# A two-layer graph network with residual norms on one core: the table of edge counts built inside the first 16 blocks of layer 0, its dense products in the next 25, staging by ScalarE and VectorE

## The reference

```python
# layer 0: graph convolution with self loops
deg  = segment_sum(1, dst) + 1;  dinv = rsqrt(deg)
h    = segment_sum(dinv[src] * dinv[dst] * (x @ W)[src], dst) + dinv**2 * (x @ W) + b
x    = layernorm(x + h + t_emb @ Wt + bt)
# layers 1 and 2: two sage convolutions, the second on relu of the first
mean = segment_sum(h[src], dst) / max(cnt, 1)
h    = mean @ Wl.T + h @ Wr.T + b
x    = layernorm(x + h2)
```

## Time and profile before

| what | value |
|---|---|
| median of 3 runs | 3074.04 us (3073.63 to 3077.73) |
| the profiled execution | 3073.91 us |
| its span, first to last instruction | 3072.1 us |
| mean granted TensorE clock | 0.965 |
| PE busy | 2648.3 us, 86% |
| POOL busy | 1972.9 us, 64% |
| DVE busy | 1115.7 us, 36% |
| ACT busy | 557.2 us, 18% |
| DMA, mean over the span | 209 GB/s |

### The profile page before, as it was taken

One profiled execution on the slowest core, in us unless ns is written; L12 is line 12 of the kernel. 1 busy time (PEld: TensorE's weight loads), 2 busy tenths in 40 slices (PEclk: granted clock), 3 DMA queues, 4 the chain that ended last, 5 costly groups with the idle time before them and its releaser, 6 DMA issues.

```text
span 3072.1 us, 53544 instructions
## 1 busy us (share of the span) xinstructions
PE 2648.3 (86%) x9848; PEld 988.0 (32%) x9849; DVE 1115.7 (36%) x2442; ACT 557.2 (18%) x1268; POOL 1972.9 (64%) x2061
## 2 busy tenths in 40 slices
PE   7567788888888988999999998988988889989988
PEld 6321222222222333333333323333333333333323
DVE  8771222334454521122223333332222223334444
ACT  0130111111222211111112112221111111222222
POOL 1247777777776646556667777746555656777774
PEclk9998999999999999999999999999999999999999
DMA  5247777777777756667778888866656667777775
GB/s 188 92 162 210 209 219 220 221 223 225 226 227 217 211 164 194 196 205 212 222 222 250 252 255 251 257 221 200 178 169 181 193 189 206 224 225 227 232 216 162
DMA packets 223328, 641.67 MB, mean 209 GB/s; under 512 B 38526, under 2 KB 40144, under 8 KB 223270
## 3 DMA queue, kind: packets, MB, share of 16 engines
q0 software_dynamic: 161280, 528.61, 59.4%
q1 hardware_dynamic: 46356, 84.02, 7.5%
q10 hardware_dynamic: 15666, 28.72, 2.8%
HBM read 589.84 MB, written 52.15 MB: 209 GB/s over the span
## 4 chain that ended last, share of the span: by engine, by line
PE 61%; issue 12%; DVE 8%; POOL 6%; DVEq 5%; DMA 5%; ACT 2%; ACTq 1%; POOLq 0%; SPq 0%
PE sum_ps L1241 26%; PE prod_ps L1235 13%; PE root_ps L1252 13%; POOL raw L534 6%; PE dense_ps L1268 4%; DMA raw<-table,idx_ring 3%; ACT half_sum L1015 2%; PE selfT_ps L1280 1%; DVE oh L875 1%; PE root_ps L1121 1%; DVE X L805 1%; DMA raw<-rows,idx_ring 1%; DVEq L318 1%; DVEq L312 1%; DVE oh_key L766 1%
## 5 line engine op out<-in xcount | busy, mean ns | idle before, releaser
L534 POOL DMA_INDIRECT raw<-rows,idx_ring x1344 | 1280.9, 953 | 692.1 <-issue 452.0
L1241 PE MATMUL sum_ps<-raw,oh 128*64 128x512 f32 x4032 | 1001.7, 618 | 145.1 <-DVE oh L875 67.7
L534 POOL DMA_INDIRECT raw<-table,idx_ring x672 | 640.5, 953 | 230.1 <-issue 183.2
L1235 PE MATMUL prod_ps<-W,aggT 128*128 128x512 f32 x1176 | 553.8, 614 | 15.1 <-issue 10.1
L1241 PEld LDWEIGHTS sum_ps<-raw,oh 128*64 128x64 f32 x4032 | 273.9, 140 | 765.2 <-issue 760.4
L1252 PE MATMUL root_ps<-W,selfT 128*128 128x512 f32 x800 | 405.9, 654 | 120.6 <-DVE X L789 67.4
L1015 ACT ACTIVATE half_sum<-sum_ps 64x512 f32<-64x512 f32 x294 | 174.4, 593 | 1234.3 <-PE sum_ps L1246 1234.3
L1241 PE MATMUL sum_ps<-raw,oh_next 128*64 128x512 f32 x1176 | 317.2, 618 | 5.9 <-DVE oh_next L854 5.7
L1235 PEld LDWEIGHTS prod_ps<-W,aggT 128*128 128x128 f32 x1176 | 218.0, 196 | 238.4 <-issue 236.2
L875 DVE TENSOR_TENSOR oh<-iota_ps,dst_rel 128x512 f32<-128x512 f32 x253 | 173.7, 687 | 311.3 <-PE sum_ps L1241 281.3
L817 DVE TENSOR_TENSOR agg<-sum_ps,half_sum 64x512 f32<-64x512 f32 x147 | 100.3, 683 | 504.5 <-ACT half_sum L1015 493.1
(11 more groups left out here) (209 smaller groups left out, 1425.2 us busy)
## 6 DMA issues: line engine op xcount, KB each, us to landing
selfbuf<-rows ACTq DMA_DIRECT2D x103, 256.0 KB
raw<-rows,idx_ring POOLq DMA_INDIRECT x1344
rows<-X SPq DMA_DIRECT2D x49, 256.0 KB
rows<-hbuf SPq DMA_DIRECT2D x49, 256.0 KB
X<-rows SPq DMA_DIRECT2D x49, 256.0 KB
out<-X SPq DMA_DIRECT2D x48, 256.0 KB
table<-stage SPq DMA_DIRECT2D x21, 512.0 KB, 3.3
raw<-table,idx_ring POOLq DMA_INDIRECT x672
```

What stands on the lines that cost most here:

```text
L534: nc.gpsimd.indirect_dma_start(out=raw[:, n, j, :], out_offset=None, in_=tables[L][:, :], in_offset=bass.IndirectOffsetOnAxis(ap=idx_ring[ ...
L1235: last = mm(product(L, t1), aggT[:, k * P:(k + 1) * P], W[:, 0, k, :], start=(k == 0), stop=(k == KD - 1))
L1241: return mm(sum_ps[j * H:(j + 1) * H, bank:bank + D], of[:, j, :], raw[:, n, j, :], start=fresh, stop=False, skip_group_check=True)
```

## The change

- The counting leaves the prologue. In each of blocks 0 to 15 of layer 0 (`i < COUNT_BLOCKS`), DVE makes and PE multiplies the batches of two windows, one before each half, into `root_ps` and `dense_ps` by turns, and ScalarE reads them out there.
- The dense products of layer 0 come in blocks 16 to 40, one before each half: 50, the last on a tile of zeros. They take `table0`'s rows (dinv·x) from `selfbuf`, which ScalarE loads by DMA, and `counts` unscaled. The table `rooted` is not read in layer 0.
- POOL stages nothing; DVE stages the 21 tiles, behind its tables of window ends, with `ranges`, `tile_end_counts`, `biases` and `column_numbers` put in between. ScalarE stages without a stop, but for the edge tables after the sixteenth of its 28 tiles.
- The scratch of the counting shares its room with the second weight matrix, now a tensor of its own (`W_right`). SP loads that matrix when the counting is over, after 24 tiles of layer 0 are stored.
- CAP goes from 32 to 23: fewer columns (161, not 216) can hold edges of the first 128 targets. The number of edges is the same.

```diff
-    CAP = 32
+    CAP = 23
+    COUNT_BLOCKS = DW // 2
+    DENSE_BLOCKS = -(-T // 2)
+    OWN0 = 2 * DENSE_BLOCKS
...
+        def early_blocks(eng, i, count_part, dense_part):
+            with eng.If(i < COUNT_BLOCKS):
+                count_part(nc.s_assert_within(i, 0, COUNT_BLOCKS - 1, skip_runtime_bounds_check_because="asked just here"))
+            with eng.Else():
+                with eng.If(i < COUNT_BLOCKS + DENSE_BLOCKS):
+                    dense_part(nc.s_assert_within((i - COUNT_BLOCKS) & 31, 0, DENSE_BLOCKS - 1,
+                                                  skip_runtime_bounds_check_because="asked just here"))
+                eng.nop()
+            eng.nop()
...
# SP
-            load_weights(1, wr1t, "wr_loaded")
+            with sp.Fori(0, T // 2) as t:
+                store_x(t)
+            sp.wait_ge(S["c_taken"], DW + 2)
+            load_weights(1, wr1t, "wr_loaded")
...
# POOL: its staging loop is gone
             b0 = first_block(pool)
             pool.wait_ge(S["b0_all_ps"], 1)
+            pool.wait_ge(S["ranges_made"], 1)
+            pool.wait_ge(S["tabs_made"], 2)
...
# DVE
+            for n, (first, many) in enumerate(TWOS):
+                b = first // BT
+                if b >= 2 and first % BT == 0:
+                    dve.wait_ge((S["stage_stored0"], S["stage_stored1"])[b % 2], 16 * PAIRS * (b // 2))
+                if many == 2:
+                    t = first + 1
+                    v.tensor_scalar(stage[:, b % 2, t % BT, :], X[:, t, :], dinv[:, t:t + 1], None,
+                                    ALU.mult).then_inc(S["staged_dve"], 1)
+                if n == 8:
+                    ranges()
+                if n == 10:
+                    tile_end_counts()
+                if n == 16:
+                    biases()
+                if n == 20:
+                    column_numbers()
             relative_targets()
...
+            def count_edges(i, half):
+                first = dense_bounds(mybir.EngineType.DVE, dense_first, i * 2 + half)
+                shift = dense_bounds(mybir.EngineType.DVE, dense_shift, i * 2 + half)
+                batches(dve, first[0], first[1], lambda g: dense_batch(i * 2 + half, g, shift[0]))
...
                     for half in range(2):
                         if L > 0:
                             each(dve, rounds[half], rounds[half + 1], lambda r: own_rows(L, r), T + 1)
+                        else:
+                            with dve.If(i < COUNT_BLOCKS):
+                                count_edges(...)
+                            dve.nop()
                         each(dve, ends[half], ends[half + 1], window_end)
                         half_block(...)
...
                     dve.wait_ge(S["stage_stored1"], 16 * 3 * PAIRS)
+                    dense_columns()
...
# ScalarE, in each half of layer 0's blocks
+                    def taken(i):
+                        take_counts(i * 2 + half, (root_ps, dense_ps)[half])
+                        if half == 1:
+                            with act.If(i > COUNT_BLOCKS - 2):
+                                first_counts()
+                            act.nop()
+                    def ahead(d):
+                        if half == 0:
+                            tile_ahead(d * 2 + 1)
+                        else:
+                            with act.If(d < DENSE_BLOCKS - 1):
+                                tile_ahead(d * 2 + 2)
+                            act.nop()
+                    early_blocks(act, i, taken, ahead)
...
+            def next_tile(t1):
+                act.dma_start(selfbuf[:, :], table0[rows_of(t1), :]).then_inc(S["self_loaded"], 16)
+                next_counts(t1)
+            def tile_ahead(done):
+                act.wait_ge(S["dense_done"], done)
+                next_tile(...)
...
# PE, in each half of layer 0's blocks, ahead of its four groups
+            def count_window(w, bank, first, end):
+                pe.wait_ge(S["c_taken"], w + 1)
+                clear(bank, KEYS)
+                batches(pe, first, end, lambda g: count_pairs(bank, g))
+                mm(bank[:, 0:1], zeros[:, :], zeros[:, 0:1], start=False, stop=True,
+                   skip_group_check=True).then_inc(S["c_ready"], 1)
...
+            def first_layer_dense(d, half):
+                t1 = d * 2 + (1 + half)
+                pe.wait_ge(S["self_loaded"], t1 * 16)
+                pe.wait_ge(S["cbuf_ready"], t1)
...
+                    add_dense(selfbuf[:, :], False).then_inc(S["dense_done"], 1)
```

More of the change, by code:

```diff
@@ L1022, in own_rows @@
                 act.dma_start(selfbuf[:, :], rows32[L - 1][rows_of(r + 2), :]).then_inc(S["self_loaded"], 16)
-                next_counts(nc.s_assert_within(r + 2, 1, CTILES, skip_runtime_bounds_check_because="two tiles ahead"), L)
-            def first_layer_counts(r):
-                with act.If(r < T):
-                    act.wait_ge(S["dense_done"], r)
-                    next_counts(nc.s_assert_within(r + 1, 1, T, skip_runtime_bounds_check_because="not the last tile"), 0)
-                act.nop()
+                next_counts(nc.s_assert_within(r + 2, 1, CTILES, skip_runtime_bounds_check_because="two tiles ahead"))
             def deviation(L, t1):
@@ L1234, in weigh @@
                 for k in range(KD):
-                    last = mm(product(L, t1), aggT[:, k * P:(k + 1) * P], W[:, 0, k, :], start=(k == 0),
+                    last = mm(product(L, t1), aggT[:, k * P:(k + 1) * P], W[0][:, k, :], start=(k == 0),
                               stop=(k == KD - 1))
@@ L1251, in by_weights @@
                 for k in range(KD):
-                    last = mm(out_ps, xT[:, k * P:(k + 1) * P], W[:, n, k, :], start=(k == 0),
+                    last = mm(out_ps, xT[:, k * P:(k + 1) * P], W[n][:, k, :], start=(k == 0),
                               stop=(k == KD - 1))
@@ L1268, in add_dense @@
                 return mm(dense_ps[:, :], cbuf[:, :], rows, start=fresh, stop=False, skip_group_check=True)
-            def first_layer_dense(r):
-                with pe.If(r < T):
-                    t1 = nc.s_assert_within(r + 1, 1, T, skip_runtime_bounds_check_because="not the last tile")
-                    pe.wait_ge(S["cbuf_ready"], t1)
-                    add_dense(tile_of_x(t1), False).then_inc(S["dense_done"], 1)
-                pe.nop()
+            def first_layer_dense(d, half):
+                t1 = d * 2 + (1 + half)
+                pe.wait_ge(S["self_loaded"], t1 * 16)
+                pe.wait_ge(S["cbuf_ready"], t1)
+                if half == 0:
+                    with pe.If(d > 0):
+                        add_dense(selfbuf[:, :], False).then_inc(S["dense_done"], 1)
+                    with pe.Else():
+                        add_dense(selfbuf[:, :], True).then_inc(S["dense_done"], 1)
+                    pe.nop()
+                else:
+                    add_dense(selfbuf[:, :], False).then_inc(S["dense_done"], 1)
             def transpose_own(rows):
@@ L1301, in _, with first_layer_half, count @@
                         transpose_own(selfbuf)
+                def first_layer_half(i, half):
+                    def count(i):
+                        first = nc.values_load_multi_w_load_instructions(
+                            dense_first[0:1, bass.ds(i * 2 + half, 2)], engines=[mybir.EngineType.PE], min_val=0, max_val=GMAX,
+                            skip_runtime_bounds_check_because="counts of batches, bounded by the capped number of edges")[1]
+                        count_window(i * 2 + half, (root_ps, dense_ps)[half], first[0], first[1])
+                    early_blocks(pe, i, count, lambda d: first_layer_dense(d, half))
                 def groups(i, b):
                     ends = ended_before(mybir.EngineType.PE, b * SLOTS, SLOTS)
-                    rounds = rooted_before(mybir.EngineType.PE, b)
+                    if L > 0:
+                        rounds = rooted_before(mybir.EngineType.PE, b)
                     for n in range(SLOTS):
-                        if n % HR == 0:
-                            each(pe, rounds[n // HR], rounds[n // HR + 1],
-                                 first_layer_dense if L == 0 else lambda r: own_rows(L, r), T + 1)
+                        if n % HR == 0 and L > 0:
+                            each(pe, rounds[n // HR], rounds[n // HR + 1], lambda r: own_rows(L, r), T + 1)
+                        elif n % HR == 0:
+                            first_layer_half(i, n // HR)
                         group(i, n, ends[n], ends[n + 1])
```

203 lines of the change are left out of this document (93 added, 110 removed).

## The result

| | before | after |
|---|---|---|
| median | 3074.13 us (3073.63 to 3077.73, 4 runs) | 3045.97 us (3044.08 to 3048.67, 4 runs) |
| profiled execution, its span | 3073.91, 3072.1 us | 3044.08, 3042.0 us |
| mean granted clock | 0.965 | 0.961 |

The ratio after to before is 0.9907, 95% interval [0.9894, 0.9919]: about 28 us faster. The forecast was 48 us faster.

What follows compares the result with a forecast made beforehand. It took the prologue to be held by ScalarE's staging between counts, layer 0 by POOL's gathers, layers 1 and 2 by PE. 3073.9 − 63 + 2 + 11 + 2 = 3025.9 us, forecast 3026, range 3004 to 3055.

Steps and rivals of the forecast that it cites:

- part 2: Counting inside blocks 0 to 15 of layer 0: +2 us, between 0 and +10.
- part 3: Dense products in blocks 16 to 40 of layer 0: +11 us, bounds 0 and +40.
- part 1: Prologue: counting leaves, staging runs at the DMA's pace, first gather at 152 instead of 215.0: −63 us, −70 to −45.
- rivals A and B: A: late products find no cover, 3042 to 3055, chance 0.14; B: staging stays chained, 3046 to 3056, chance 0.08.
- rival D: Blocks 0 to 15: DVE-PE-DVE hand-off makes blocks longer than POOL's 19.6 us; chance 0.05 slower (3112), 0.05 part (3045 to 3068).
- The walk: Prologue: double buffer followed through seven groups of four stores; table complete at 151 to 152, first gather at 152.
- step 2: The sum's term for counting inside blocks 0 to 15: +2 us, with no charge for contention between DVE and POOL.
- Rival C: Blocks 0 to 15: DVE's counting batches lengthen POOL's gathers, about 31 us, giving 3057; chance 0.03.
- Rival A: Late blocks of layer 0: dense products find no cover in PE's waits, 3042 to 3055; chance 0.14.
- Part 4: Layer 0's dense products: the tile now comes by DMA, loaded half a block ahead; cost 0.
- Part 5: Branches and reads on DVE and PE, counted in the late halves where DVE matters: +2 us, between −2 and +8.

Runs made afterwards that it cites:

- e4: Kernel after, with POOL instead of VectorE staging its share of the first two buffers (six tiles): 3035.89 us, ratio 0.9875 to the kernel before.
- e1: Kernel after, with VectorE making the counting batches one half ahead, before the current half's window end: 3026.30 us, ratio 0.9832 to the kernel before.
- e8: Kernel after, with batches one half ahead and both key and source one-hots reading their row of numbers from PSUM: 3007.30 us, ratio 0.9792 to before.
- e2: Kernel after, with only the key one-hots' row of key numbers read from PSUM instead of SBUF: 3053.76 us, ratio 0.9922 to the kernel before.
- e5: Kernel after, with batches one half ahead and the key one-hots' numbers read from PSUM: 3016.36 us, ratio 0.98 to the kernel before.
- e3: Kernel after, without 49 of the 50 dense products of layer 0, tile loads and count copies kept: 3051.24 us, one run.
- e6: Kernel after, with batches one half ahead and key one-hots made by tensor_tensor from two SBUF inputs: 3039.01 us, ratio 0.9859 to the kernel before.

## Why the prediction was right or wrong

*Direction and range:* right. The time, 3046, is in the range of 3004 to 3055, 20 us over the forecast of 3026. That remainder is one term of the sum, part 2, 37 us too low, against which part 3 was 9 us too high and part 1 was 3 us too low in its gain; the range held it because it left room for other things, late products without cover and a chained staging (rivals A and B), that did not come. In that the range was lucky: what came is rival D's "a part of it", which had 0.05.

*Part 1, −63 us:* right, −66. The first store was issued at 111.63 instead of 113.8. The last store was issued at 144.1 by 111.63 + 32.45, the first gather at 148.64 instead of 152. The walk had the ranges at 6.0 us; they took 3.2, from 118.33 to 121.58. The wait of `biases` for PE is where it was put, but ends at 131.25 us, with the copy done by 131.93, and not at 137.6; the groups of stores behind it still waited for landings, as walked:

```profile
131.25 0.68 DVE L709 COPY bin_row<-selfT_ps 1x512 f32<-1x512 f32 x1 [3.12 <-PE selfT_ps L1236]
...
137.94 1.28 DVE L769 TENSOR_SCALAR stage<-X,dinv 128x512 f32<-128x512 f32 x3 [3.77 <-DMA table<-stage]
```

e4 shows what the walk took as given, DVE's tables ahead of its first tile: 5.5 us.

*Part 2, +2 us with bounds of 0 and +10:* wrong, +39. This is the step that failed, in two of its sentences. The first: "5 us with one batch, 6.7 with two, against 9.8 us for half a POOL block". The sum added up DVE's and PE's pieces and set them against POOL's half, as if the chain could start when the half came up on POOL. It starts when DVE comes to it, and DVE comes to it only after the window end before it, which waits for ScalarE's `half_sum`, which waits for PE: 39.1 + 38.1 us of such waits in the sixteen blocks. So the counting of a half stood end to end with PE's own half, and could not run beside it. The loss fell where the prediction saw none: not so much in block 0 (22.9 us), which has eight batches where nine were expected, as in blocks 10, 11, 13 and 14, with one batch a half. One size was off too: reads and branches were put at 1.5 us, which holds for the second half of a block (1.4), while the first half takes 3.0 and more. Rival D named this place and gave 0.05 to "a part of it (3045 to 3068)"; its mark, POOL idle in blocks 0 to 15, is in the windows above. Its line "against: 5 to 7 us a half" rested on the same sum. e1 prices it at 22.1 us.

The second: "the trace shows no contention, and step 2 charges none", from 15.12 against 15.13 us of POOL's busy time. The two numbers are right and cannot carry that sentence. POOL goes from gather to gather with 0.30 us between them, so in a window of fixed length it is busy about as long whether the gathers are short or long. And of DVE's 11.36 us in the second stretch, 6.4 were instructions with an input in PSUM, such as `oh` from `iota_ps`, a kind that e8 shows to be harmless. Taken singly, the gathers of that same stretch do show it, DVE and POOL of the kernel before:

```profile
926.58 0.75 DVE L832 SCALAR_TENSOR_TENSOR agg<-X,dinv,agg 128x512 f32<-128x512 f32 x1 [0.26 <-DVE agg L826]
926.82 1.33 POOL L534 DMA_INDIRECT raw<-table,idx_ring  x1 [0.30 <-issue]
```

L832 has both inputs in SBUF and ends 0.51 us after the gather's start: 0.51 + 0.82 = 1.33. In layer 0 of the kernel before 18 gathers met it in this way, and each took its end plus 0.82 us, within 0.01. Together that is only 3.6 us, which is why no sum shows it. Equal busy times over a window are no evidence about work of the kind that is to be added. Rival C had the kind right and the price too high, 31 us against 16.5 (9.3 + 7.2); its rule in the Trainium skill (SBUF — State Buffer, "Who interferes with whom": a VectorE instruction with two SBUF inputs contends with a GpSimd instruction that reads SBUF) agrees with every run here, but for the one-hots that began just before a gather, and its mark, POOL's mean above 0.953 us, was met with 1.011. The chance of 0.03 was given against a rule that no row contradicted and that the trace bore out.

The two do not simply add: with the hand-off there, removing contention brought nothing (e2), and from e2 to e5, the other way round, the hand-off is worth 33.9 us (362.4 to 328.5) where it was worth 22.1 from the kernel after to e1. The contention is hidden behind the hand-off, so the shares hold for the order e1, e5, e8; that both are needed for the 39 us holds for either.

*Part 3, +11 us:* too high, but of the right kind. (As written, 40 − 14.6 − 15 is 10.4; with 38 × 1.06 = 40.3 it is 10.7.) Blocks 16 to 40 cost 2.0 us more than before, and the products 3.3 us by e3, where they might have cost 52. I counted 14.6 us of gather waits and 15 of one-hot waits as cover for 40 us; e3 against the kernel after shows 10.7 and 20.5 of these gone, 31 us. Of the rest, some 16 us stand against slower products in e3, at the lower clock, a term that the sum did not have. Rival A, no cover, falls.

*Part 4, 0:* right within 2.5 us: the profile shows one wait of PE for `selfbuf`, of 2.5 us, in the 25 blocks.

*Part 5, +2 us:* not tested by itself. What the branches and reads cost on DVE showed where it counts, in part 2, and the late blocks leave no room for more than the 2.0 us that they lost in all.

*Layers 1 and 2:* the lead at layer 1 was to be 48 us and is 22.8, as the blocks left it. From there to the last gather it grew by 5.6 us. No edit touches this part, and over the same stretch the lead of e1 grew by 1.8 us (44.9 to 46.6) and that of e8 by 10.7 (57.8 to 68.6). From the first gather of layer 1 to the last of all, the same instructions took from 1923.6 us (e8) to 1941.6 us (e6) in the eleven traces, with a granted clock over that stretch of 0.975 and 0.968; the others lie between, the slower ones at the lower clock in the main. That the clock is the cause is likely and not shown, and what sets it stays open. So a step of a few us is to be read from the blocks, not from the whole time.

## What to carry to other kernels

A step that is put into a loop between two engines costs its latency, not its busy time: follow it from the moment when its engine can begin, in program order, and make it one step ahead if it can be. The sixteen blocks went from 359.9 to 337.8 us by that alone. When a resource conflict is to be judged from a trace, look at single instructions beside one of the kind that is added, by its operands' places (one gather of 1.33 us was enough here), not at sums over a window; and where two costs bound the same stretch, take away the larger one before judging the other.

## What the runs showed of the hardware

- POOL's indirect DMA of 128 rows takes 0.95 us here; held by a VectorE instruction that began before it and has both tensor inputs in SBUF, it takes the time to that instruction's end plus 0.82 us, up to 1.76 us beside a one-hot of 1.03 us (38 of 38 in the kernel after, and 18 of 18 beside `agg<-X,dinv,agg` in layer 0 of the kernel before). VectorE pays nothing: L801 took 1.02 to 1.03 us beside short and long gathers alike. Tensor_tensor (e6) and scalar_tensor_tensor do it equally.
- A tensor_scalar of one SBUF tensor (L878) does it too, when it has begun more than 0.15 us before the gather: 22 of 52 gathers in the kernel after, up to 1.18 us.
- With one of the two inputs in PSUM a one-hot holds no gather: 0 of 52 in e8. The one-hots took as long from PSUM (0.69 and 1.02 us) as from SBUF (0.69 and 1.03).
- A half's table reads and branches on DVE took 1.3 to 1.7 us in the second half of a block and 3.0 to 3.6 us in the first, before the first instruction behind them (kernel after).
